# First attention of a four-stage transformer kernel: the value projection in equal rounds, one key head and 128 moving columns at a time

## The reference

```
qkv = h @ Wqkv.T                       # h: 1024 tokens (32 samples x 32) x 512
xq, xk = rope(q), rope(k);  xv = v     # 32, 8 and 8 heads of 128
scores = causal(xq @ xk.T / sqrt(128)) # within a sample
out = softmax(scores) @ xv
x = x + out @ Wo.T
```

## Time and profile before

| | |
|---|---|
| median of 3 runs | 1026.8 us (1025.46 to 1026.83) |
| the profiled execution | 1021.81 us |
| its span | 1019.7 us |
| mean granted TensorE clock | 0.991 of full speed |
| TensorE busy | 966.5 us, 95% of the span |
| first attention, from the first key/query tile (L1133) on | from 106.35 us of the span |

### The profile page before, as it was taken

The page is one execution under the profiler, slowest core; times in us unless marked ns, Lnnn a source line. Parts: engine busy times, 40 slices in busy tenths (PEclk is TensorE's granted clock), DMA queues, the critical chain, the costliest instruction groups (busy, mean ns, idle before and its releaser), DMA issues.

```text
span 1019.7 us, 15772 instructions
## 1 busy us (share of the span) xinstructions
PE 966.5 (95%) x6686; PEld 695.8 (68%) x6686; DVE 554.2 (54%) x947; ACT 229.2 (22%) x443; POOL 458.9 (45%) x417
## 2 busy tenths in 40 slices
PE   6899989999999999999999789989989999899997
PEld 2338877778888788777887578738845556446853
DVE  7856739475384835648376434434147968302323
ACT  4602022221302212111210200110161655500001
POOL 7935548584675837578275403202112434320300
PEclk9999999999999999999999899999999999999999
DMA  5782102011111011211014092694340000072002
GB/s 136 184 238 67 55 1 79 36 42 53 43 73 42 3 50 42 73 42 53 1 42 124 1 215 86 136 195 161 131 186 1 2 2 3 1 158 70 4 1 83
DMA packets 36286, 74.29 MB, mean 73 GB/s; under 512 B 13492, under 2 KB 22260, under 8 KB 33140
## 3 DMA queue, kind: packets, MB, share of 16 engines
q1 hardware_dynamic: 35880, 72.89, 25.6%
q10 hardware_dynamic: 336, 0.39, 0.1%
HBM read 66.26 MB, written 7.01 MB: 72 GB/s over the span
## 4 chain that ended last, share of the span: by engine, by line
PE 72%; DVE 10%; POOL 7%; DMA 4%; ACT 3%; issue 3%; SPq 1%; POOLq 0%; DVEq 0%; ACTq 0%
PE ps L1133 14%; PE ps L1195 12%; PE ps L994 8%; PE ps L1439 5%; PE ps L1267 5%; PE ps L1372 5%; PE ps L1147 4%; POOL w_lo L2307 3%; DVE arena L1973 3%; DMA arena<-level_rows 2%; ACT acts L1484 2%; DVE arena L1970 2%; PE ps L1393 1%; PE ps L1272 1%; PE ps L1399 1%
## 5 line engine op out<-in xcount | busy, mean ns | idle before, releaser
L2413 POOL TENSOR_TENSOR arena<-arena 128x512 f32<-128x512 f32 x80 | 103.5, 1295 | 123.1 <-DVE arena L1973 123.0
L1133 PE MATMUL ps<-xt_hi,w_hi 128*128 128x512 f32 x320 | 127.9, 400 | 5.8 <-POOL w_lo L2307 2.7
L1133 PE MATMUL ps<-xt_lo,w_hi 128*128 128x512 f32 x320 | 125.6, 392 | 0.0
L1133 PE MATMUL ps<-xt_hi,w_lo 128*128 128x512 f32 x320 | 125.0, 391 | 0.0
L1195 PE MATMUL ps<-h_hi,wo_hi 128*128 128x512 f32 x256 | 104.9, 410 | 11.9 <-DVE h_lo L1982 11.9
L1991 DVE TENSOR_TENSOR fresh<-ps,fresh 128x512 f32<-128x512 f32 x56 | 38.7, 692 | 133.7 <-PE ps L1195 133.6
L1973 DVE TENSOR_TENSOR arena<-ps,rope 64x512 f32<-64x512 f32 x160 | 110.2, 689 | 2.2
L1195 PE MATMUL ps<-h_lo,wo_hi 128*128 128x512 f32 x256 | 103.1, 403 | 0.0
L1195 PE MATMUL ps<-h_hi,wo_lo 128*128 128x512 f32 x256 | 102.3, 400 | 0.0
L2330 POOL TENSOR_TENSOR xt<-arena 128x512 f32<-128x512 f32 x24 | 30.5, 1270 | 137.0 <-DVE arena L1878 137.0
L1577 ACT ACTIVATE h_hi<-ps 128x512 fp32r<-128x512 f32 x64 | 33.0, 603 | 203.1 <-PE ps L1180 203.1
(11 more groups left out here) (313 smaller groups left out, 1804.0 us busy)
## 6 DMA issues: line engine op xcount, KB each, us to landing
acts<-in_w_o_dram SPq DMA_DIRECT2D x8, 1024.0 KB, 4.9
arena<-in_a_wo_dram SPq DMA_DIRECT2D x8, 1024.0 KB, 5.7
arena<-kernel_rows SPq DMA_DIRECT2D x11, 512.0 KB, 11.3
acts<-in_w_qkv_dram SPq DMA_DIRECT2D x3, 1792.0 KB, 7.3
acts<-in_w_qkv_dram SPq DMA_DIRECT2D x4, 1280.0 KB, 6.6
w_l<-kernel_rows SPq DMA_DIRECT2D x10, 512.0 KB, 11.9
arena<-level_rows SPq DMA_DIRECT2D x4, 1024.0 KB, 21.3
stream<-in_x_dram SPq DMA_DIRECT2D x4, 512.0 KB, 6.7
```

What stands on the lines that cost most here:

```text
L1133: last = pe.matmul(ps[:, bank, :], w[:, r, cols], x, start=(r == 0 and n == 0), stop=(r == R - 1 and n == 2))
L2413: pool.tensor_tensor(qk[:, chunk, half * HALF:(half + 1) * HALF], rot[:, k % 2, 0, :], rot[:, k % 2, 1, :], ALU.add).then_inc(s_rope, 1)
```

## The change

The values of one key head are computed in each round, with 128 moving columns. `values(i)` now fills 2 PSUM tiles of 4 token blocks; it is called for every i. For rounds 1 to 6 it stands at the place that the even ones had; `values(7)` stands in round 6 between `keys_queries(7)` and the first projection tile. Each round loads, rounds and splits 768 columns of weights. (The host's layout still has 7 blocks, and round 0 still loads all of them.) The waits and the plan of the ring follow.

```diff
         def wcols(i):
-            return WPART if i % 2 == 0 else 5 * HD
+            return 6 * HD
...
             if i == NKV - 2:
                 kq_tiles(i + 1, range(8, 10))
+                for v in range(2):
+                    ring_tile(("v", i + 1, v), s_v, 2 * (i + 1) + v + 1)
...
-            for v in range(4 if i % 2 and i + 1 < NKV else 0):
+            for v in range(2 if i < NKV - 2 else 0):
...
                 def values(i):                                   # TensorE
-                    for v in range(4):
+                    for v in range(2):
                         bank = ring(("v", i, v))
-                        for m in range(2):
-                            tile = 2 * v + m
+                        for m in range(4):
+                            tile = 4 * v + m
                             for r in range(R):
                                 x_hi = xt_hi[:, r, tile * P:(tile + 1) * P]
                                 x_lo = xt_lo[:, tile, r, :]
                                 for n, (x, w) in enumerate(((x_hi, w_hi), (x_hi, w_lo), (x_lo, w_hi))):
-                                    last = pe.matmul(ps[:, bank, m * 2 * HD:(m + 1) * 2 * HD], x,
-                                                     w[:, r, 5 * HD:7 * HD],
+                                    last = pe.matmul(ps[:, bank, m * HD:(m + 1) * HD], x,
+                                                     w[:, r, 5 * HD:6 * HD],
...
                 def pv(i, half):
-                    pe.wait_ge(s_v, 4 * (i // 2) + 4)
+                    pe.wait_ge(s_v, 2 * i + 2)
...
                         keys_queries(i + 1, range(8, 10))        # round 6
+                        values(i + 1)
                         project(i, range(2))
...
-                    if more and i % 2:                           # rounds 0 to 5
+                    if more:
                         values(i + 1)
...
                 def values(i, tiles):                            # ACT
                     for v in tiles:
                         act.wait_ge(s_vt, 2 * i + v + 1)
-                        if i:
-                            act.wait_ge(s_pv, 2 * i)
-                        act.activation(vals[:, :, 2 * v:2 * v + 2, :], ...
+                        if i >= 2:
+                            act.wait_ge(s_pv, 2 * i - 2)
+                        act.activation(vals[:, i % 2, 4 * v:4 * v + 4, :], ...
...
                 def round_qkv(i):
                     act.wait_ge(s_qkv, 10 * i)
-                    act.wait_ge(s_vt, 4 * ((i - 1) // 2) + 4)
+                    act.wait_ge(s_vt, 2 * i)
...
                     round_heads(i, 0)
+                    if i == NKV - 2:
+                        values(i + 1, range(2))
                     round_heads(i, 1)
-                    if i % 2 and i + 1 < NKV:
-                        values(i + 1, range(4))
+                    if i < NKV - 2:
+                        values(i + 1, range(2))
```

More of the change, by code:

```diff
@@ L1538, in values @@
                         act.wait_ge(s_vt, 2 * i + v + 1)
-                        if i:
-                            act.wait_ge(s_pv, 2 * i)
-                        act.activation(vals[:, :, 2 * v:2 * v + 2, :],
-                                       ps[:, ring_at["v", i, v], :].rearrange("p (m h d) -> p h m d", m=2, h=2),
+                        if i >= 2:
+                            act.wait_ge(s_pv, 2 * i - 2)
+                        act.activation(vals[:, i % 2, 4 * v:4 * v + 4, :],
+                                       ps[:, ring_at["v", i, v], :].rearrange("p (m d) -> p m d", m=4),
                                        ACT.Copy).then_inc(s_v, 1)
@@ L1577, in round_heads @@
                         act.activation(dst, src, ACT.Copy).then_inc(s_hhi, 1)
-                values(0, range(4))
+                values(0, range(2))
                 round_qkv(1)
```

## The result

The changed kernel takes 1063.8 us (median of 4 runs, 1063.4 to 1065.5) against 1026.8 us: a ratio over all runs of 1.037, 95% interval 1.0344 to 1.0397 (the two medians are 36.9 us, 3.6%, apart). The forecast was 1064.6 us, in a range of 1058 to 1072.

A forecast was written before the change was run, and what follows sets the result against it. TensorE, busy for 95% of the span, was taken to bound the kernel. Groups +42.4, pauses -5.8 and first round +1.2 made +37.8 us: 1059.6 profiled, 1064.6 us with the 5.0 to the median kept, range 1058 to 1072.

The forecast's parts named there:

- What a group costs: Value matmuls on TensorE: 768 of 128 columns at 112 ns each, 86.0 us in place of 43.6, +42.4 us.
- the open load behind a pause: After TensorE's 3.26 us idle at 564.08, a rounded weight load stood unhidden for 109 to 110 ns.
- the 64-column stream: Unrounded matmuls with 64 moving columns, 110 ns apart, read as a floor of one 128x128 weight load.
- The pauses: TensorE's 1.93 us pauses behind rounds without values, three pairs, go once each round has a values group: -5.8 us.
- The first round: POOL's four wider pieces for round 1 and ACT's first lie uncovered on the chain: +1.2 us.
- What costs nothing: ACT's read-outs, weight transfers, `values(7)` at round 6's 3.26 us pause, and the work behind the attention add no time.
- the wait for POOL's zeros: Behind the attention, the next convolution waits for these, then a 23.56 us transfer; all moves with the rounds, nothing won or lost.
- The distance to the median: The median of runs lay 5.0 us above the profiled execution; kept, it turns 1059.6 into 1064.6 us.
- The sum: Groups +42.4, pauses -5.8, first round +1.2: +37.8 us in all.
- Hidden: Rival: the weight load hides behind rounded matmuls at 128 columns too; -4.4 us, 1022.4 us; chance 0.05.
- half hidden loads: Rival: value matmuls 84.5 ns apart, midway between 57 and 112; +16.7 us, 1043.5 us; chance 0.05.
- load and matmul in series: Rival: no overlap in the value groups, 167 ns a matmul; +80.1 us, 1106.9 us; chance 0.06, slower still included.

The follow-up runs named there:

- e5: Changed kernel with 256 moving columns in each value matmul, the second head's result thrown away, as many matmuls: 1067.6 us.
- e3: Changed kernel with one product (rounded with rounded) in place of three in the values, both corrections left out: 1006.2 us, ratio 0.981.
- e2: Kernel before with each value matmul of 256 moving columns made as two of 128, still two heads every second round: 1067.0 us, ratio 1.040.
- e1: Changed kernel with each value matmul of 128 moving columns made as two of 64, same result: 1279.6 us, ratio 1.247.
- e4: Kernel before with POOL's second convolution blocks of even rounds moved into odd rounds, both ahead of the weight splitting there: 1020.0 us, ratio 0.994.
- e8: The changed kernel itself, run again beside the others on the same chip with a second profile: 1063.4 us.
- e6: Changed kernel with only 640 columns of weights loaded, rounded and split in round 1, head 1's values made with stale weights: 1060.4 us.
- e10: Changed kernel with as many value matmuls, each of 64 moving columns, the lower half of each value head written twice: 1113.4 us.

## Why the prediction was right

- **What a group costs.** The step was: half the columns buy nothing, since the stream has a floor at one weight load; 112 ns, bounds 110 and 114. Measured 111 ns (10.67 us for 96), 41.8 us for all in place of 42.4, well inside the bounds. The reading of the two rows it rested on holds: the open load behind a pause, 110 ns, and the 64-column stream that did not go below 110 ns. But the 64-column stream showed the floor for unrounded operands alone, and for rounded ones a single open load had to speak; the runs made it firm. e5 shows the columns hidden behind the loads, e3 and e2 that the price follows the count of pairs, and e1, while its clock was full, that it is not a slower rate. That it is not the issuing of a pair is shown by the 29 ns of the scores with their 128x32 loads.
- **The pauses.** The step was that all 5.8 us go. They do, but for 0.04 us a round: rounds of 65.29 us against 65.25 of pure work. That POOL's own order made them was argued from the masks; e4 shows it.
- **The first round.** 1.2 us by the sum, 1.2 at full clock (e8, e6). What the sum had no term for is a lower clock behind the wait, 0.9 us in one profile and none in another (e8).
- **What costs nothing.** `values(7)` behind the pause of 3.26 us: the pause is there as it was, 3.25 us ahead of the projection at 603.63. The transfers never show in the chain of the rounds. Behind the attention the forecast had the wait for POOL's zeros and the transfer of the earlier trace rows move along, and this part did not come: the chain now goes through the last projections and the convolution's matmuls, without that transfer. It cost the forecast little, for before TensorE waited only 0.6 us for the landing:

```profile
L994 PE MATMUL ps<-w_l,stream 128*128 128x128 f32 x256 | 40.0, 279 | 0.6 <-DMA arena<-level_rows 0.6
```

- **The distance to the median** was taken as the 5.0 us of the profile of before. It goes with the higher clock of that one execution (0.991, where the others have 0.982 to 0.988) and is no property of the kernel: the profile after lies 1.8 us above its median, not 5.0 below, and at 1065.5 us it is 5.9 above the 1059.6 named for its like. Keeping the distance amounts to adding the sum to the old median, and that is what came out.
- **The sum.** At full clock the attention is 37.4 us longer (495.12 in e8 against 457.73), where the sum had 37.8: the groups were taken 0.6 too dear, the pauses 0.3 too large. The medians are 36.9 apart. That the median met the forecast within 0.8 us is closer than the spread of 2 us and more among the runs of either kernel allows to count on; the terms, each within 0.6 us, are the better proof.
- **The rivals.** Hidden and half hidden loads would be groups of 5.5 and 8 us; load and matmul in series, 16. None of it is in the trace. The 81 ns a matmul of the Trainium skill (TensorE: Matmul & The Clock Gate, Back-to-back issue gap) is not reached by any stream of rounded 128-column loads here: 110 to 111 ns. The rule of the Trainium skill for the load itself (the same page, LDWEIGHTS), 107 ns, is 4 ns short of the distance in e1 and in the changed kernel.

## What to carry to other kernels

Count weight loads as well as columns: where each matmul has its own 128x128 load, narrowing it below 256 moving columns saved nothing here (111 ns at 128 and 114 at 256, rounded operands), and splitting a two-head product doubles its price. Equalising stages can be worth something, but ask first who is late in the unequal ones; here another order of work on POOL gave the same 5.8 us with no matmul added (e4). And a change that widens what a stage writes can take away an early start that the narrow stage allowed.

## What was not expected of the hardware

A stream of matmuls that never idles can lose its clock. With 64 moving columns and a load of 128x128 for each, the granted clock fell to 0.50 within each group (e1, e10), where the same stream with 128 columns kept 1.00; the distance of two matmuls went from 111 to 214 ns. Why 64 columns lower the clock is open. Fewer columns for the same loads made the kernel 50 us slower (1113.4 against 1063.4).
